# AdaLN block with chunked ridge attention and an FP4 feed-forward: the triangle of each pivot chain handled problem by problem, the feed-forward output turned on TensorE, a shorter orthogonalisation and rounding

## What is computed

```python
h = _layernorm(x) * (1 + ca) + sa
x = x + ga * attn(h)
h = _layernorm(x) * (1 + cb) + sb
x = x + gb * ffn(h)
```

```python
G = Kc.T @ Kc + RIDGE_EPS * I
W = jnp.linalg.solve(G, Kc.T @ Vc)
U = I[:, :8]
for _ in range(2):
    U, _ = jnp.linalg.qr(W @ U)
Wr = U @ (U.T @ W)
S_new = 0.9 * S + Wr
out = 0.125 * (Qc @ S_new)
```

```python
h = jax.nn.silu(fp4_linear(x, w_gate)) * fp4_linear(x, w_up)
return fp4_linear(h, w_down)
```

## Time and profile before

| | us |
|---|---|
| median of 3 runs | 1487.51 |
| lowest and highest of them | 1479.54, 1488.72 |
| the profiled execution | 1489.35 |
| its span (first to last instruction) | 1487.5 |
| busy in the span: DVE | 1230.2 |
| PE | 969.3 |
| ACT | 640.3 |
| POOL | 231.3 |

### The profile page before, as it was taken

One profiled execution on the slowest core, in us unless ns is written; L12 is line 12 of the kernel. 1 busy time (PEld: TensorE's weight loads), 2 busy tenths in 40 slices (PEclk: granted clock), 3 DMA queues, 4 the chain that ended last, 5 costly groups with the idle time before them and its releaser, 6 DMA issues.

```text
span 1487.5 us, 43627 instructions
## 1 busy us (share of the span) xinstructions
PE 969.3 (65%) x17726; PEld 780.0 (52%) x17726; DVE 1230.2 (83%) x3729; ACT 640.3 (43%) x1294; POOL 231.3 (16%) x149
## 2 busy tenths in 40 slices
PE   1443940389177799787799787852819825996175
PEld 0332530365167667677667686742717624775154
DVE  5885659949999779996799996798875798878997
ACT  3663630156135466555466454431416512563152
POOL 3552001101111001113102023012140000021000
PEclk9855985589579899899899898785959957898597
DMA  2555110001000001001101002030030200111000
GB/s 78 168 167 194 46 44 0 1 18 50 8 4 4 4 10 46 2 4 50 54 17 38 3 4 86 4 123 0 4 125 19 75 1 17 50 47 32 9 25 24
DMA packets 52086, 61.60 MB, mean 41 GB/s; under 512 B 4048, under 2 KB 32416, under 8 KB 51888
## 3 DMA queue, kind: packets, MB, share of 16 engines
q1 hardware_dynamic: 51888, 58.84, 12.6%
HBM read 38.31 MB, written 20.51 MB: 40 GB/s over the span
## 4 chain that ended last, share of the span: by engine, by line
DVE 36%; PE 32%; issue 13%; ACT 5%; POOL 2%; DMA 1%; SPq 0%; DVEq 0%; POOLq 0%; ACTq 0%
PE a_bank L840 5%; PE a_bank L830 3%; PE a_bank L846 3%; DVE a_total L1581 3%; DVE a_outer L1579 3%; DVE a_blocks L1584 3%; DVE a_outer L1575 2%; PE a_bank L946 2%; PE a_bank L961 2%; PE a_bank L769 2%; PE a_bank L898 2%; PE a_bank L698 2%; DVE a_blocks L1586 2%; DVE a_recip L1561 2%; PE a_bank L808 2%
## 5 line engine op out<-in xcount | busy, mean ns | idle before, releaser
L1092 ACT ACTIVATE a_work<-a_bank 128x512 f32<-128x512 f32 (+1 forms) x193 | 110.9, 599 | 206.5 <-PE a_bank L808 170.8
L1485 POOL TENSOR_TENSOR a_root<-a_recip,a_half 128x32 f32<-128x32 f32 (+2 forms) x24 | 89.8, 3743 | 655.8 <-DVEq L1570 636.9
L808 PE MATMUL a_bank<-a_ident,a_blocks 128*128 128x128 f32 x256 | 42.2, 340 | 162.6 <-DVE a_blocks L1595 162.6
L1092 ACT ACTIVATE a_solve<-a_bank 128x512 f32<-128x512 f32 (+2 forms) x184 | 87.9, 522 | 114.1 <-PE a_bank L846 53.9
L1575 DVE TENSOR_TENSOR a_outer<-a_blocks,a_weight 128x62 f32<-128x62 f32 (+15 forms) x248 | 129.4, 522 | 0.0
L1581 DVE TENSOR_REDUCE a_total<-a_outer 128x62 f32<-128x62 f32 (+30 forms) x248 | 127.0, 512 | 0.3
L808 PEld LDWEIGHTS a_bank<-a_ident,a_blocks 128*128 128x128 f32 x256 | 40.4, 208 | 163.7 <-DVE a_blocks L1595 163.7
L1579 DVE TENSOR_TENSOR a_outer<-a_blocks 128x60 f32<-128x60 f32 (+14 forms) x240 | 119.2, 497 | 0.7 <-DVE a_outer L1575 0.7
L1584 DVE TENSOR_TENSOR a_blocks<-a_blocks,a_outer 128x60 f32<-128x60 f32 (+14 forms) x240 | 118.3, 493 | 0.0
L698 PE MATMUL a_bank<-a_wk,a_cg 128*128 128x512 f32 x256 | 117.3, 602 | 0.0
L769 PE MATMUL a_bank<-a_scaled,a_blocks 128*128 128x352 f32 x256 | 90.6, 495 | 28.7 <-ACT a_scaled L1072 15.2
(11 more groups left out here) (200 smaller groups left out, 2402.4 us busy)
## 6 DMA issues: line engine op xcount, KB each, us to landing
f_x<-in_L_attn_x SPq DMA_DIRECT2D x16, 256.0 KB, 3.2
s_xnt<-f_xt SPq DMA_DIRECT2D x16, 256.0 KB, 2.1
s_c<-f_cm SPq DMA_DIRECT2D x16, 256.0 KB, 2.3
s_base<-f_base SPq DMA_DIRECT2D x16, 256.0 KB, 2.8
a_cg<-s_c SPq DMA_DIRECT2D x16, 256.0 KB, 2.9
a_cc<-s_c SPq DMA_DIRECT2D x16, 256.0 KB, 3.7
a_xnt<-s_xnt SPq DMA_DIRECT2D x16, 256.0 KB, 3.9
a_base_in<-s_base SPq DMA_DIRECT2D x13, 256.0 KB, 2.6
```

The lines of the kernel that those rows point to most:

```text
L808: last = nc.tensor.transpose(bank[:, i * P:(i + 1) * P], rows_[:, :, 4 * rb + i], ident[:])
L1092: nc.scalar.activation(out, view, ACT.Copy, scale=scale).then_inc(emptied, 1)
L1485: nc.gpsimd.tensor_tensor(root[:, :, a:b], recip[:, :, a:b], half[:, :, a:b], ALU.pow).then_inc(roots_ok, 1)
```

## The change

1. **factor.** The triangle has a tile of its own (`triangle`, x by columns). It is cleared before the blocks are waited for (`given`). `weight` is gone: the negative scaled columns, which `column` has stored as rows of m, are the weights, and `known` reads them as `m[:, :, 0:i, i]`. Products and additions of the triangle are made for each problem s apart: product(0) behind `known`, product(1) behind the sums, add(0) between the corrected column and its reciprocal, add(1) in the next link between column and `known`. They take in row j of the identity, so they are i rows long and not j. The clearing behind the chain is gone, and one product with the roots makes all of m.
2. **orthogonalise.** The dots of the vector with itself and the rest are made in one product and one sum, the dots are scaled by the reciprocal, and one product over both problems is subtracted.
3. **fp4_blocks.** Mask and a bitwise or in one instruction, maximum and addition in one, maximum and subtraction in one: nine steps become eight.
4. **Feed-forward output.** down(b) is cut into turn_hidden(b) and down(b). down(b) now makes the output turned (w_dn is the stationary operand, 512 columns at once), ScalarE scales it by gb (a column, as channels are on the partitions), and TensorE adds the residual x by a product with the identity and turns yt back by products with it. finish is gone. The gb rows are loaded once, by a DMA more ahead of turn_rows, and turned.
5. **Order of steps.** g0 g1, then t(b) g(b+2) y(b) for each b, where it was g(b+1) d(b).

```diff
@@ fp4_blocks
-    each(lambda v, amax, scale, inv, step: V.tensor_scalar(step.bitcast(I32), v.bitcast(I32), 0x7F800000, None, ALU.bitwise_and))
-    each(lambda v, amax, scale, inv, step: V.tensor_scalar(step, step, 1.0, 1.5 * 2.0 ** 22, ALU.max, ALU.mult))
-    each(lambda v, amax, scale, inv, step: V.tensor_tensor(v, v, step, ALU.add))
-    each(lambda v, amax, scale, inv, step: V.tensor_tensor(v, v, step, ALU.subtract))
+    each(lambda v, amax, scale, inv, step: V.tensor_scalar(step.bitcast(I32), v.bitcast(I32), EXPONENT, LARGE, ALU.bitwise_and, ALU.bitwise_or))
+    each(lambda v, amax, scale, inv, step: V.scalar_tensor_tensor(v, step, ROUNDER, v, ALU.max, ALU.add))
+    each(lambda v, amax, scale, inv, step: V.scalar_tensor_tensor(v, step, ROUNDER, v, ALU.max, ALU.subtract))
...
@@ Tensor.down
+                self.u.need(self.at["hht"])
+                bank = self.u.fill()
+                for k, (at, n) in enumerate(FI_CHUNKS):
+                    last = nc.tensor.matmul(bank[:], w_dn[0:n, k], hht_[0:n, k], start=(k == 0), stop=(k == NW - 1))
+                self.done(last)
                 m = self.u.mark()
                 yield
+                if b < EARLY:
+                    self.pe.wait_ge(x_in[b % 3], 16 * len(range(b % 3, b + 1, 3)))
+                bank = self.u.fill()
+                nc.tensor.matmul(bank[:], ident[:], x.rearrange("p t d -> p (t d)"), start=True, stop=False, skip_group_check=True)
                 self.u.need(m)
-                bank = self.u.fill()
                 for t in range(NC):
-                    for k, (at, n) in enumerate(FI_CHUNKS):
-                        last = nc.tensor.matmul(bank[:, t * P:(t + 1) * P], hht[0:n, k, t], w_dn[0:n, k], start=(k == 0), stop=(k == NW - 1))
+                    last = nc.tensor.matmul(bank[:, t * P:(t + 1) * P], yt[:, t * P:(t + 1) * P], ident[:], start=False, stop=True,
+                                            skip_group_check=True)
...
@@ Scalar.down
+                bank = self.u.empty()
+                nc.scalar.activation(yt, bank[:], ACT.Identity, scale=gb[:, b:b + 1]).then_inc(emptied, 1)
...
@@ last_group
-            steps = [("g", 0)] + [(kind, b + (kind == "g")) for b in range(B - 1) for kind in "gd"] + [("d", B - 1)]
+            steps = [("g", 0), ("g", 1)] + [(kind, b + 2 * (kind == "g")) for b in range(B) for kind in "tgy" if kind != "g" or b + 2 < B]
...
@@ factor
+                    ch.link(V.memset(triangle[:], 0.0))
+                    ch.inc(V.memset(ones, 1.0))
+                    dve.wait_ge(*given)
                     ch.link(V.tensor_scalar(diagonal, diagonal, RIDGE_EPS, None, ALU.add))
...
                         ch.wait(inverse)
...
-                        weights = ch.inc(V.scalar_tensor_tensor(weight[:, :, 0:i], m[:, :, i, 0:i], -1.0, recip[:, :, 0:i], ALU.mult, ALU.mult))
                         column = ch.inc(V.scalar_tensor_tensor(m[:, :, j, i:HB], m[:, :, i:HB, j], -1.0, bcast(recip[:, :, j], 2, n_i), ALU.mult, ALU.mult))
-                        ch.wait(weights)
-                        terms = area(0, n_i, i)
-                        known = ch.inc(V.tensor_tensor(terms, m[:, :, i:HB, 0:i], bcast(weight[:, :, 0:i], 2, n_i), ALU.mult))
                         if j:
-                            ch.wait(column)
-                            step = area(2 * KEPT * KEPT, j, n_i)
-                            product = ch.inc(V.tensor_tensor(step, bcast(m[:, :, j, i:HB], 2, j), bcast(row, 3, n_i), ALU.mult))
+                            ch.wait(second)
+                            added[1] = ch.inc(add(1, j, before))
+                        ch.wait(column)
+                        known = ch.inc(V.tensor_tensor(terms, m[:, :, i:HB, 0:i], bcast(m[:, :, 0:i, i], 2, n_i), ALU.mult))
...
+                        first_ = product(0)
                         ch.wait(known)
                         summed = ch.inc(V.tensor_reduce(total[:, :, 0:n_i], terms, op=ALU.add, axis=AX_X))
-                        if j:
-                            ch.wait(product)
-                            ch.inc(V.tensor_tensor(rest, rest, step, ALU.add))
+                        second = product(1)
                         ch.wait(summed)
-                        ch.link(V.tensor_tensor(m[:, :, i:HB, i], m[:, :, i:HB, i], total[:, :, 0:n_i], ALU.add))
+                        corrected = ch.inc(V.tensor_tensor(m[:, :, i:HB, i], m[:, :, i:HB, i], total[:, :, 0:n_i], ALU.add))
+                        ch.wait(first_)
+                        added[0] = ch.inc(add(0, i, step))
+                        ch.wait(corrected)
                         inverse = pivot(i)
...
-                    for i in range(1, HB):
-                        V.memset(m[:, :, i, 0:i], 0.0)
-                    ch.link(V.memset(diagonal, 1.0))
+                    ch.wait(second)
+                    ch.link(add(1, HB - 1, before))
                     dve.wait_ge(roots_ok, n * 3)
-                    V.tensor_tensor(m[:, :, 0:KEPT], m[:, :, 0:KEPT], bcast(root[:], 2, KEPT), ALU.mult)
-                    V.tensor_tensor(m[:, :, KEPT:HB, KEPT:HB], m[:, :, KEPT:HB, KEPT:HB], bcast(root[:, :, KEPT:HB], 2, KEPT), ALU.mult).then_inc(done, 1)
+                    V.tensor_tensor(m, x, bcast(root[:], 2, HB), ALU.mult).then_inc(done, 1)
```

126 lines of the change are left out of this document (65 added, 61 removed).

## The result

The changed kernel took 1503.09 us (median of four runs, 1500.29 to 1505.79), the kernel before 1488.12 beside it: a ratio of 1.0112, with a 95% interval of 1.0074 to 1.0150. It is slower, by 15.0 us where 16.5 were forecast. The two profiled executions are 12.4 us apart (1501.73 and 1489.35, spans 1499.9 and 1487.5), and that difference can be split by stage. Start times are read from VectorE's timeline; quantise(b) stands for the start of its first product (L1636 before, L1679 after), and (3) for quantise(3).

The account below looks back on a forecast made before the run. VectorE's five factorisations on the path and its late batches bound the kernel, woven TensorE work the stage between. Factorisations +32, leading blocks +2.2, feed-forward part -17.7 gave +16.5, so 1504.0 us; own range 1492 to 1516, overall 1466 to 1528.

Parts of the forecast that it names:

- The stride: Known product in each factorisation: elements read 128 bytes apart cost about 1.6 cycles, +6.8 us a factorisation.
- stride for free: Rival: the long known product streams at one cycle, feed-forward gains remain, 1468 us; chance 0.22.
- half rate: Rival: two cycles an element in the known product, +11.0 us a factorisation, 1535 us; chance 0.08.
- Waits and count: Factorisation links: one direct wait fewer, one instruction more, -0.06 us a link, -1.9 us in all.
- The end: End of a factorisation: removed memsets give nothing as POOL releases the scaling; two scalings become one, +0.5 us.
- Slack of the leading blocks: Leading blocks beside TensorE's subspace stage: group 0 passes its 6.1 us slack, +2.2; groups 1 and 2 nothing, over 10.
- The orthogonalisation: Vector steps on VectorE get shorter, -3.7 us in all, counting only in group 3; net -1.
- starts some 2.7 us later: Group 3's orthogonalise delayed because the woven stage before it also holds gate_up(3), 5 us more TensorE work.
- the late batches and the tail: Feed-forward end: batches 10 to 15 shorten on VectorE, -11.9 us; the last batch, -1.
- combine_last's contention: POOL's combine_last moves beside quantise(9) and stands on the path, +5 us.
- The hidden pass 0: Hidden-input pass ahead of the first gate loses one element-wise step on VectorE, -1.3 us.
- TensorE bounds the late stage: Rival: TensorE at the lower clock in half the late batches takes back the whole 17.7 us, 1522; chance 0.10.

Follow-up runs that it names:

- experiment 4: Changed kernel with the known product's second operand read from consecutive addresses, its sum not added to the column, so values differ: 1460.42 us (0.9801).
- experiment 5: Changed kernel with the earlier factorisation (contiguous weights tile), its products and additions split by problem: 1439.19 us (0.9699).
- experiment 2: Kernel before with the new factorisation alone, plus the changed kernel's smaller DMA scratch setting: 1529.40 us (1.0296).
- experiment 8: Changed kernel with the earlier factorisation, and each batch's output put ahead of the gate of the batch after next: 1468.64 us (0.9914).
- experiment 10: Kernel of experiment 5 with the feed-forward weights' row loads issued after the second, not fourth, of POOL's combined batches of group 2: 1420.91 us (0.9554).
- experiment 3: Changed kernel with weights computed again into a contiguous tile that the known product reads, one instruction more a link: 1469.30 us (0.9877).
- experiment 6: Kernel before with the shorter rounding alone, three element-wise steps in place of four: 1472.02 us over ten runs (0.9929).

## Why the prediction was right, point by point

- **The stride** was the term that decided: +6.8 us a factorisation, from two short forms. In lead(0) the group L1624 is busy 23.2 us where L1575 was 16.2, +7.0, and experiment 4 takes it away: the "stride for free" and "half rate" rivals are out. The prediction took one price for all five factorisations, and that was too small for three: lead(0) and schur(3) grew by 6.1 and 6.3 us, schur(0) to (2) by 7.0 to 7.5; that makes +34.3 of +32. Only part of this is the stride (L1624 is busy 23.5 to 24.0 us there). Experiment 4, without the stride, takes 1.0 us more in schur(0) to (2) than in lead(0) as well, where before takes 0.3 more; most of the 1.0 is that two of the columns (L1619) are followed by the next instruction 0.3 to 0.4 us later. Other engines work beside these three, and they are also the ones that the kernel runs in its loop over the groups; which of the two does it wasn't tried.
- **Waits and count** (-1.9) measured -2.1 in experiment 4. Its rule of 0.13 us for a wait and 0.07 for an instruction would give 31 x 2 x 0.06 = 3.7 us for the two waits of experiment 5, which brought 2.9 to 3.6.
- **The end** (+0.5) is +0.47, and POOL releases L1643 as before.
- **Slack of the leading blocks**: +2.2 was forecast for group 0 and nothing for groups 1 and 2. From schur(0)'s end to schur(1)'s start it is +2.9. The slack of the other two was read too large: in before's trace the leading blocks of groups 2 and 3 are done at 689.8 and 901.6 us and TensorE turns them at 698.93 and 910.31, which is 9.2 and 8.7 us and not over 10. After the change TensorE waits 1.31 us for those of group 2. Ahead of group 2's Schur blocks the stretch is +2.2, but the wait there is 1.31 us and experiment 2 has none; the granted clock of its last 48 us is 0.74 (0.84 in before's last 45), and over the twelve other profiles it is anything from 129.7 to 134.5 us. The leading blocks don't account for it, and what sets it wasn't tried. The other stretches give 2.7 back (-1.7 before schur(0), -1.3 before schur(3), +0.3 before lead(0)).
- **The orthogonalisation** is shorter by 3.9 (3.7 forecast). The step that failed is "starts some 2.7 us later". It starts 0.15 us earlier, counted from quantise(0). The timelines of ScalarE and of VectorE before, and of VectorE after:

```profile
1172.47 1.09 ACT L1092 ACTIVATE a_basis<-a_bank 128x512 f32<-128x512 f32 x2 [0.80 <-PE a_bank L985]
```

```profile
1180.14 0.69 DVE L1654 TENSOR_TENSOR a_blocks<-a_blocks 128x512 f32<-128x512 f32 x1
1180.74 0.28 DVE L1611 TENSOR_TENSOR a_outer<-a_basis 128x128 f32<-128x128 f32 x1
```

```profile
1216.76 1.23 DVE L1662 TENSOR_TENSOR a_outer<-a_basis 128x1024 f32<-128x1024 f32 x1 [12.15 <-ACTq L1135]
```

  The basis was there at 1173.6, and VectorE came to it 7.2 us later, out of quantise(2) and finish(1). After, quantise(2) is done early and VectorE waits 12.15 us for a basis that TensorE's longer weave brings 7.0 us later, counted from quantise(0) (50.4 us behind it, where it was 43.5). The bound changed sides, and the 7.2 us of room took up the 7.0. Experiment 8 bears it out: with gate_up(3) behind the output again, the basis is there 44.0 us after quantise(0) and VectorE comes to it at 49.1 without waiting. I had charged TensorE's work and not looked at how long the basis had lain there. This is 3.0 of the 6.5 us by which the feed-forward part beat its forecast (-24.2 against -17.7).
- **The other terms**: the late batches and the tail gave 14.0 (12.9 forecast, the tail at full clock -2.7, of which I took -1), the TensorE stage 2.8 (1.0), which is no more than the spread of that stage in the profiles with the old output (83.4 to 86.7 us). combine_last's contention from quantise(9) to (10) is real but 4 us and not 5, by experiment 8. The hidden pass 0 gave no part of its 1.3: experiment 10 shows what that stretch hangs on, and over the twelve profiles without it its length is 90.7 to 100.4 us, a spread wider than the term.
- **Right by luck in part**: the factorisations cost 2.4 us more than forecast and the feed-forward gave 6.5 more, errors of opposite sign, so the sum was 4 us high against the profiles' 12.4. That the medians are 15.0 us apart, closer to the forecast, is the runs' spread: their interval allows 11 to 22 us.
- **TensorE bounds the late stage** didn't happen in the changed kernel, and 12 us a batch for TensorE against 11.3 for VectorE was the right sum (12.43 and 11.31). Experiment 8 shows that the step order, g between t and y, is what makes it enough: the other order costs 15.8 us there. In experiment 3 the rival came in part: a stretch at the lower clock used up the lead, and the late stage took 2.8 us more.

## What to carry to other kernels

An instruction saved by reading a result where it lies is paid for when it lies one element to a 16-byte piece: 2·i·n_i elements at 0.63 cycle were 7 us, the tile that avoids it 3. Splitting independent problems to fill the waits of a chain works, 0.05 to 0.07 us for each wait filled, and is best done with the operands left contiguous. And before charging an engine's added work to a step, look how long that step's input had lain ready.

## What the runs showed of the hardware that I had not expected

- The price of distance is a step and not a slope: none at 8 bytes, half at 12, all of it from 16 bytes on, the same at 132. It isn't paid either where the operand's inner run is only two or three elements, read again and again: L1624 with 174 elements takes 0.33 us at i = 3 and 0.44 at i = 29 (0.33 at both in experiment 4), and the full price is there from i = 4 on (224 elements: 0.53 us against 0.38). If the two problems' values lay side by side, 8 bytes together, the strided operand might be free; that wasn't tried.
- POOL and VectorE hold each other up by whole instructions. POOL's product of 512 elements takes 1.27 us where none of VectorE's long products with two inputs runs, and 3.22 beside two of them, of which the second takes 3.23 us and the first 2.29. In the timelines of before, POOL's ends 1.12 us after L180 does, and L181, started at 1083.88, ends 2.1 us after POOL's:

```profile
1074.97 1.27 POOL L1492 TENSOR_TENSOR a_xc<-a_xc,a_ga 128x512 f32<-128x512 f32 x1
...
1081.75 3.22 POOL L1492 TENSOR_TENSOR a_xc<-a_xc,a_ga 128x512 f32<-128x512 f32 x1 [4.15 <-DMA a_ga<-s_mod]
```

```profile
1081.56 2.29 DVE L180 TENSOR_TENSOR a_solve<-a_solve,a_blocks 128x2048 f32<-128x2048 f32 x1
1083.88 3.23 DVE L181 TENSOR_TENSOR a_solve<-a_solve,a_blocks 128x2048 f32<-128x2048 f32 x1
```

  The Trainium skill (SBUF — State Buffer, section SBUF: two separate sides) calls the pair's shared port an exclusive lock; the trace agrees. How the instructions of the two fall against each other differs from run to run, and in the stretch ahead of quantise(0), where POOL's combines are the path, that goes with lengths of 90.7 us (experiment 6, POOL's second product 1.37 us) to 100.4 (experiment 2, 3.06); from the start of the first of POOL's eight products to the end of the last it is 24.9 us in experiment 6 and 31.5 in experiment 2. That it is the cause of the spread of 6 to 21 us in a kernel's times is likely and wasn't shown.
